# A state-space scan on one core: replication layout, a ring of two blocks, and a re-timed side schedule

## The reference, cut to what matters

```
x, z   = split(hidden @ in_proj.T)            # 512 channels each
u      = silu(conv4(x) + conv_b)              # causal, 4 taps
dt,B,C = split(u @ x_proj.T)                  # 16, 16, 16
delta  = softplus(dt @ dt_proj.T + dt_b)
dA     = exp(delta[..., None] * A)            # 512 channels x 16 states
dBu    = delta[..., None] * B[:, :, None, :] * u[..., None]
h      = dA * h + dBu                         # along 512 tokens
y      = sum_n(h * C)                         # over the 16 states
out    = ((y + u * D) * silu(z)) @ out_proj.T
```

## Time and profile before

| | us |
|---|---|
| median of 3 runs | 2438.59 |
| the profiled execution | 2434.86, with a span of 2433.1 |
| VectorE busy in the span | 1505.5 (62%) |
| TensorE (matmul) | 1817.2 (75%) |
| ScalarE, GpSimd | 1001.6 (41%), 941.8 (39%) |
| granted TensorE clock, mean | 0.838 |

### The profile page before, as it was taken

One profiled execution on the slowest core, in us unless ns is written; L12 is line 12 of the kernel. 1 busy time (PEld: TensorE's weight loads), 2 busy tenths in 40 slices (PEclk: granted clock), 3 DMA queues, 4 the chain that ended last, 5 costly groups with the idle time before them and its releaser, 6 DMA issues.

```text
span 2433.1 us, 21744 instructions
## 1 busy us (share of the span) xinstructions
PE 1817.2 (75%) x6696; PEld 770.0 (32%) x6696; DVE 1505.5 (62%) x1744; ACT 1001.6 (41%) x1542; POOL 941.8 (39%) x676
## 2 busy tenths in 40 slices
PE   6588989899999898761775766848758658478566
PEld 6344444435353535130212213213122122132212
DVE  6364646464656464411875876858768767587596
ACT  3134344343435252523453462543534534536332
POOL 2500000000000000104675675755756756556563
PEclk9899999999999999975777967869779668688666
DMA  4663544535252535116309036063090270540800
GB/s 173 201 134 59 130 67 120 78 109 90 97 99 88 99 100 90 57 42 146 71 18 206 12 80 153 10 142 83 10 207 18 61 174 10 125 91 1 202 14 9
DMA packets 104592, 223.80 MB, mean 92 GB/s; under 512 B 14177, under 2 KB 66530, under 8 KB 100818
## 3 DMA queue, kind: packets, MB, share of 16 engines
q1 hardware_dynamic: 101458, 214.69, 38.0%
q0 software_dynamic: 3072, 8.37, 1.0%
HBM read 169.56 MB, written 53.48 MB: 92 GB/s over the span
## 4 chain that ended last, share of the span: by engine, by line
PE 14%; issue 11%; DVE 10%; POOL 7%; POOLq 7%; DMA 5%; ACT 1%; DVEq 1%; SPq 1%; ACTq 0%
DVE ps L1440 6%; PE ps L1532 4%; POOL work L1181 4%; DMA rep<-rep_rows 3%; PE ps L1563 3%; DVE work L1446 3%; PE ps L1555 2%; POOLq L1152 2%; POOLq L1221 1%; POOL xn L1156 1%; PE ps L1565 1%; PE ps L1525 1%; DMA bc<-bc_rows 1%; POOLq L1168 1%; POOLq L1170 1%
## 5 line engine op out<-in xcount | busy, mean ns | idle before, releaser
L1440 DVE TENSOR_TENSOR_SCAN ps<-ps,work 128x1024 f32<-128x1024 f32 x256 | 586.3, 2290 | 318.7 <-POOL work L1181 282.4
L1181 POOL TENSOR_TENSOR work<-rep,bc 128x1024 f32<-128x1024 f32 x256 | 599.3, 2353 | 441.4 <-PE ps L1555 314.2
L1555 PE MATMUL ps<-work,pick 128*32 128x512 f32 x1024 | 325.9, 792 | 362.1 <-DVE work L1446 362.0
L1316 ACT ACTIVATE ps<-rep,a_neg 128x512 f32<-128x512 f32 x512 | 332.4, 681 | 640.2 <-DVE work L1446 599.0
L702 DVE TENSOR_REDUCE m<-ps 128x1 f32<-128x512 f32 x512 | 327.6, 686 | 163.6 <-PE ps L808 161.9
L625 ACT ACTIVATE prob<-ps 128x1024 f32<-128x1024 f32 x256 | 256.7, 1021 | 236.1 <-PE ps L832 234.0
L1446 DVE TENSOR_TENSOR work<-ps,bc 128x1024 f32<-128x1024 f32 x256 | 308.6, 1206 | 0.0
L1532 PE MATMUL ps<-xn_t,in_taps 128*128 128x510 f32 (+3 forms) x512 | 235.1, 615 | 13.4 <-ACT u L1254 12.4
L566 POOL TENSOR_TENSOR m_parts<-m,nil 128x16 bf16<-128x16 f32 x32 | 7.1, 222 | 604.0 <-DVE m L702 604.0
L808 PE MATMUL ps<-k_st,q_st 96*128 96x512 bf16 x512 | 184.6, 407 | 57.0 <-DMA k_st<-qk_parts 34.8
L1555 PEld LDWEIGHTS ps<-work,pick 128*32 128x32 f32 x1024 | 37.9, 121 | 590.9 <-DVE work L1446 526.9
(11 more groups left out here) (176 smaller groups left out, 1990.7 us busy)
## 6 DMA issues: line engine op xcount, KB each, us to landing
rep<-rep_rows SPq DMA_DIRECT2D x128, 512.0 KB, 16.0
w<-in_w SPq DMA_DIRECT2D x32, 1024.0 KB
rep_rows<-inputs SPq DMA_DIRECT2D x32, 512.0 KB, 6.3
bc<-bc_rows SPq DMA_DIRECT2D x128, 128.0 KB, 17.8
qk_parts<-parts SPq DMA_DIRECT2D x96, 128.0 KB
q_st<-qk_parts SPq DMA_DIRECT2D x96, 128.0 KB, 10.3
k_st<-qk_parts SPq DMA_DIRECT2D x96, 128.0 KB, 11.1
dispatch<-zeros SPq DMA_DIRECT2D x4, 1280.0 KB, 10.6
```

Source lines behind the costliest of these rows:

```text
L1181: nc.gpsimd.tensor_tensor(work[:, n % WS, :, :], rep[:, c, 2 * h:2 * h + 2, 1, :], bc[:, k, 0, :].unsqueeze(1).broadcast_to([P, 2, SEQ]), ...
L1316: e = nc.scalar.activation(state(n)[:, i, :], rep[:, c, 2 * h + i, 0, :], ACT.Exp, scale=a_neg[:, c, 2 * h + i, k:k + 1])
L1440: nc.vector.tensor_tensor_scan(s, s, work[:, n % WS, :, :].rearrange("p i t -> p (i t)"), 0.0, ALU.mult, ALU.add).then_inc(state_ready, 1)
L1555: x = nc.tensor.matmul(ps[j * CH:(j + 1) * CH, YB, :], pick[:, :], work[:, n % WS, i, :], start=False, stop=(n % PER_CHUNK >= PER_CHUNK - 2))
```

## The change

The tables get new positions and the kernel changes in these ways:
- **Layout.** Partition p now holds channel p // 4 and state group p % 4, so `pick` is `repeat` instead of `tile`, and each DMA of a load writes all 128 partitions. A load of `bc` is one DMA instead of four.
- **Ring.** `rep` has 2 blocks (`RS`) instead of 4. The load of chunk g waits until chunk g-2 has been used, and the loads stand in SP's queue at other places.
- **Drive places.** `WS` is 8 instead of 4.
- **Sums.** `sum_states(k)` takes pieces 2k and 2k+1 together, with one wait and one signal.
- **Halves.** The 8 matmuls of a chunk of `x` stand as 4 at q and 4 at q+1; the output projection goes by 4 tiles instead of 2 pairs.
- **Side chain.** Gather, weighing, adding, statistics and root of a batch are done one batch earlier (for b+2), so that the normalisation stands at q = 0. During batch 0, which has no such lead, all the positions are moved on by `LATE` = 5.
- **Attention.** `turn_rows(1)` and four of the second expert's eight `hide` stand ahead of the wait for `stacked`.

```
-WS = 4
+WS = 8
+RS = 2
+LATE = 5
+AHEAD = 4
...
-PE_AT = {"out": (1, 3), ... "turn_x": (6, 7), "x": (8, 10, 12, 14), "bc": 17, "dt": (19, 20, 21, 22), "z": (23, 24, 25, 26), ...
+PE_AT = {"turn_x": (0, 1), "out": (2, 3, 5, 6), ... "x": (7, 9, 11, 13), "bc": 16, "dt": (18, 19, 20, 21), "z": (22, 23, 24, 25), ...
-ACT_AT = {... "x": (11, 13, 15, 17), "silu_u": 17, ... "softplus": 24, ... "silu_z": 30}
+ACT_AT = {"normalise": 0, ... "x": (10, 12, 14, 16), "silu_u": 16, ... "softplus": 22, ... "silu_z": 29, "weigh": 24}
+DVE_AT = {"max": 2, "binade": 6, "statistics": 26}
+POOL_AT = {"down": 9, "grid": 14, "up": 17, "gather": 23, "add": 27, "input": 28, "root": 31}
...
                 def load_quad(f, k):
-                    for i in range(QUADS):
-                        n = QUADS * k + i
-                        sp.dma_start(bc[i * CH:(i + 1) * CH, k, :, :].rearrange("p r t -> p (r t)"),
-                                     rows[n:n + 1, :].broadcast_to([CH, 2 * SEQ])).then_inc(bc_loaded[k], 16)
+                    sp.dma_start(bc[:, k, :, :].rearrange("p r t -> p (r t)"),
+                                 rows.unsqueeze(0).broadcast_to([CH, QUADS, 2 * SEQ])).then_inc(bc_loaded[k], 16)
...
                 def load_inputs(f, c):
+                    g = f * DC + c
                     sp.wait_ge(rep_stored[c], f * 16 + 16)
-                    for i in range(QUADS):
-                        sp.dma_start(rep[i * CH:(i + 1) * CH, c, :, :, :].rearrange("p j r t -> p j (r t)"),
-                                     io["rep"][f % 2, c].rearrange("(j p) x -> p j x", p=CH)).then_inc(rep_loaded[c], 16)
+                    if g >= RS:
+                        sp.wait_ge(decay_ready, (g - RS + 1) * PER_CHUNK)
+                        sp.wait_ge(drive_ready, (g - RS + 1) * PER_CHUNK)
+                    for j in range(BLOCKS):
+                        rows = io["rep"][f % 2, c, j * CH:(j + 1) * CH, :]
+                        sp.dma_start(rep[:, g % RS, j, :, :].rearrange("p r t -> p (r t)"),
+                                     rows.unsqueeze(1).broadcast_to([CH, QUADS, 2 * SEQ])).then_inc(rep_loaded[g % RS], 16)
...
-                        pool.wait_ge(summed, n - WS + 1)
+                        pool.wait_ge(summed, (n - WS) // 2 + 1)
...
-                def sum_states(n):
-                    pe.wait_ge(read_ready, n + 1)
-                    for i in range(2):
-                        j = 2 * (n % 2) + i
-                        x = nc.tensor.matmul(ps[j * CH:(j + 1) * CH, YB, :], pick[:, :], work[:, n % WS, i, :], ...
+                def sum_states(k):
+                    pe.wait_ge(read_ready, 2 * k + 2)
+                    for n in (2 * k, 2 * k + 1):
+                        for i in range(2):
+                            j = 2 * (n % 2) + i
+                            x = nc.tensor.matmul(ps[j * CH:(j + 1) * CH, YB, :], pick[:, :], work[:, n % WS, i, :], ...
...
-"pick": np.tile(np.eye(CH, dtype=np.float32), (BLOCKS, 1))
+"pick": np.repeat(np.eye(CH, dtype=np.float32), QUADS, axis=0)
```

More of the change, by code:

```diff
@@ L866, in sequence @@
                         expert_out(0, j, range(HC))
+                        if j == 0:
+                            turn_rows(1)
+                    for h in range(AHEAD):
+                        hide(1, h)
                     pe.wait_ge(set_up, 1)
@@ L1007, in mix_block @@
         rep_stored = [sem(f"rep_stored_{c}") for c in range(DC)]
-        rep_loaded = [sem(f"rep_loaded_{c}") for c in range(DC)]
+        rep_loaded = [sem(f"rep_loaded_{c}") for c in range(RS)]
         dt_done = sem("dt_done")
@@ L1098, in _ @@
                 load(2)
-                spread(0)
+                store_rows(0)
+                for k in range(QUADS):
+                    load_quad(0, k)
+                for c in range(DC):
+                    store_inputs(0, c)
+                    if c == 0:
+                        load_inputs(0, 0)
                 for b in range(BATCH + 1):
+                    if b < BATCH:
+                        load_inputs(b, 1)
                     if b:
@@ L1385, in _ @@
                                 copy_quant(f, k)
-                        if q == ACT_AT["silu_z"]:
+                        if q == min(ACT_AT["silu_z"] + late, PIECES - 1):
                             silu_z(f)
@@ L1526, in in_proj, with in_proj_taps @@
                     x.then_inc(done, 1)
-                def in_proj_taps(bank, c, done):
-                    for s in range(TAPS):
+                def in_proj_taps(bank, c, taps, done):
+                    for s in taps:
                         for k in range(KD):
@@ new lines, in out_proj @@
+                def out_proj(b, t):
+                    o = ps[:, TB, (t % 2) * DM:(t % 2) * DM + DM]
+                    for c in range(DC):
+                        nc.tensor.matmul(o, sz[:, b % 2, c, t * P:(t + 1) * P], out_w[:, c, :], start=(c == 0), stop=False)
+                    for k in range(KD):
+                        nc.tensor.matmul(o, quant_t[:, b % 2, k, t * P:(t + 1) * P], fw_t[:, k, :], start=False, stop=False)
+                    nc.tensor.matmul(o, one_row, bias, start=False, stop=False)
+                    x = nc.tensor.matmul(o, sb["ident"][:, :], x2[:, b % XS, t, :], start=False, stop=True)
+                    if t % 2:
+                        x.then_inc(out_done, 1)
```

248 lines of the change are left out of this document (126 added, 122 removed).

## The result

The changed kernel takes 2224.4 us (median of 4 runs, 2220.3 to 2227.2) against 2438.1 us for the kernel before on the same chip: a ratio of 0.912, 95% interval 0.910 to 0.914. It is 214 us faster; 234 were forecast. The profiled execution took 2220.3 us with a span of 2218.5, which answers to the 2433.1 of the earlier trace rows.

The account below looks back on a forecast made before the run. VectorE was taken as the floor, busy 118.1 of 163.3 us a middle batch. Savings of 163 + 23 + 8 + 18 + 22 = 234 from 2434.9 gave 2201, 2205 with the median's 3.7; range 2152 to 2285.

Parts of the forecast that it names:

- attention: First part of the kernel: side work fills the wait for `stacked`, 2.8 us less a batch, 22 in 8 batches.
- the start: Second layer's first scan: `bc` loaded before the inputs are ready, first scan at 1134 instead of 1152, 18 us less.
- batch 0: Second layer's first batch: 17 us of late decays, gates and its end, so 135 us for 157.9, 23 less.
- six middle batches: Second layer: VectorE's 118.1 us plus 18 of stalls, 136 us a batch instead of 163.3, 163 less in six.
- head start: Attention, from the end of `expert_out` to the first probability matmul: 33.0 us instead of 35.8.
- at VectorE's pace: Attention's five steps without side work: set by two maxima of 0.69 us each, 7.0 us in all.
- attention gives nothing back: Rival: VectorE or the maxima's way through memory sets the end of the attention steps; 2227 us, chance 0.08.
- The walk: Piece-by-piece count of VectorE's stalls along a middle batch at 3.32 us a piece: late decays and gates, 18 us together.
- The drive waits: VectorE ahead of scans: 34.6 us a batch, 21 mid-batch and 13.6 at its end, go with 8 places and earlier loads.
- The seam: Batch end: first scan 15 us after the first store instead of 35, VectorE having 25 us of pieces; the stall goes.
- the ring: Rival: loads wait for a free block and each of 31 comes 9 us late; 2484 us, slower, chance 0.02.
- Halves: Chunks of `x` on TensorE: from batch 1 on no sum stands between the halves, so they cost and bring nothing.

Follow-up runs that it names:

- experiment 1: The changed kernel with the attention's second-expert output spread thinner, a quarter tile a step instead of a half: 2184.3 us, ratio 0.896.
- Experiment 2: The changed kernel with the attention's TensorE order of before, transposes and all `hide` behind the wait for `stacked`: 2223.9 us, ratio 0.913.
- experiment 4: The changed kernel with six drive places instead of eight, sums still in pairs: 2255.2 us, ratio 0.925.
- experiment 5: The changed kernel with the sums of one piece at a time instead of pairs, still eight drive places: 2257.8 us, ratio 0.927.
- experiment 3: The changed kernel with the old layout, each load of `rep` and `bc` writing 32 partitions, four loads a chunk: 2248.6 us, ratio 0.923.
- experiment 6: The kernel before with only the new layout, each load of `rep` and `bc` writing 128 partitions: 2368.2 us, ratio 0.973.
- experiment 7: The changed kernel with every chunk of `x` in one TensorE task instead of halves at q and q+1: 2227.1 us, ratio 0.914.

## Why the prediction was right, and where it was not

The parts of the sum, predicted and read from the two traces (spans 2433.1 and 2218.5):

| | predicted | measured |
|---|---|---|
| attention | -22 | -0.9 |
| the start | -18 | -20.4 |
| batch 0 | -23 | -18.9 |
| six middle batches | -163 | -166.4 |
| last batch | -8 | -8.9 |
| the tail | 0 | +0.8 |

- **Attention: the step that failed.** The prediction had the wait for `stacked` go, and the head start 2.8 us shorter; both came true (it was 4.65 us at the first probability matmul, in part since the five steps without side work took 6.0 us and not 7.0). What failed is the step from there to the sum, "22 in 8 batches", which lets the lead of the head start last to the end of the batch. The steps "at VectorE's pace" are steps in which TensorE idles, and after them its rows are those of the half clock for some 13 us (384.06 to 397.4), which gives the lead back: 0.9 us measured for the 22, which alone is as much as the 20 us by which the forecast is off. My bounds for this part went from nothing to 40 us "if the clock gains"; that it could lose did not come into the sum. The rival "attention gives nothing back" (2227 us) named the outcome and nearly the time, but by luck: it put it down to VectorE or the way through memory, and experiment 1 shows that neither held the batch. Experiment 2 confirms the size: nothing.
- **Middle batches: right in kind, and in size partly by luck.** Six at 135.6 us, 136 predicted. The walk had 1.9, 6.1, 7.2, 1.7 and 1.1 us; measured are 1.36, 5.61, 7.12, 3.98 and 1.13, with a gate at q = 17 of 1.17 that it lacked. The gate at q = 25 was mis-sized: TensorE waits at `z` for ScalarE, and I had counted only the projection. ScalarE and TensorE in this stretch:
```profile
1500.70 1.91 ACT L1306 ACTIVATE inputs<-inputs 128x2048 f32<-128x2048 f32 x1
1502.63 1.28 ACT L1333 ACT_TABLE_LOAD   x1
1503.92 2.52 ACT L1333 ACTIVATE ps<-rep,a_neg 128x512 f32<-128x512 f32 x4
1506.38 1.69 ACT L1252 ACTIVATE e_rows<-e_rows,gate_cur 128x256 f32<-128x256 f32 x4
1507.98 0.57 ACT L1310 ACTIVATE sz<-ps 128x512 f32<-128x512 f32 x1
...
1508.60 3.78 PE L1552 MATMUL ps<-xn_t,in_z 128*128 128x512 f32 x4 [6.82 <-ACT sz L1310]
```
Between the logarithm (L1306) and the copy of `z` (L1310) stand a table load, two decays and `weigh` (L1252, at q = 24), which is 1.7 us of the 6.8; no run moves `weigh`. That makes 20.4 us of stalls for 18.0, and VectorE's busy time is 2.3 us lower than I took it, 1.3 of them in the TENSOR_SCALAR. The errors cancel, and that the six batches come out within half a us of the forecast each owes something to it.
- **The drive waits went with the places**, as argued: none at 8, 19.0 us for `drive` and 20.8 for GpSimd's `to_grid` over the layer at 6 (experiment 4), 282.4 for `drive` at the 4 of the kernel before, where the order of the side work differs too. Of the pairs I had said that they save about half of the sums' TensorE time; experiment 5 finds the 16 us a batch, and that they act by `decay` and the gates.
- **The seam: right, and covered twice.** With the layout of before in the changed kernel (experiment 3) VectorE waits for `drive` at one seam of the seven, 8.7 us behind batch 0, where the changed kernel waits 7.1 for `decay`; so the new order of the loads and GpSimd's lead cover the seam without the layout; the new layout alone in the kernel before (experiment 6) takes 73 us off the waits for `drive`. The new order of the loads was not run without the lead. Loads in the new layout run at about 341 GB/s by experiment 3 and 366 by experiment 6, under the 389 that I took and well over 204. The Trainium skill, page "SBUF — State Buffer", section "Door 1: The DMA port swizzle", has 32 partitions reach half of the ports; 341 to 204 is a factor of 1.7, somewhat under its two. With a landing of 6.1 us the ring did not decide: in the changed kernel GpSimd waits for a `rep` load once, 2.5 us ahead of the first drive, and 19.8 us in nine times for `bc`, which its lead covers.
- **Halves: right**, nothing (experiment 7).
- **Batch 0: mis-sized.** 22.7 us of stalls for 17: 0.5 at scan 1, 5.6 in the gate at q = 17, 5.1 and 4.3 at scans 22 and 28, 7.1 at its end. The walk had the same two scans and the end, and one gate more.
- **Not shown: how the 214 us split.** Undone one by one, the layout is worth 24 us, two of the four new places 31 and the pairs 33, the attention and the halves nothing. The ring of two blocks, the side chain one batch earlier, and the new positions were never undone alone, so what they and the other two places brought is open.

## What to carry to other kernels

A wait that is taken away from TensorE is worth what the rows behind it show, not its length: look whether the freed time leaves it with steps that idle briefly, and at the rows behind them, where the same work cost 1.06 for 0.60 us here; spreading the same side work over nearly all steps turned 0 into 40 us, though two batches of eight still fell to the lower clock. Where several engines hand a side chain around under one bound engine, put a long ScalarE task and its neighbours at different places, and put TensorE tasks that wait for ScalarE behind the sums that the bound engine needs next. A change that brings nothing alone (the logarithm apart) may be worth 16 us once the wait that takes it back is gone, so try it again after each step.

## What the runs showed of the hardware

**TENSOR_SCALAR of VectorE waits inside itself for GpSimd.** No list of waits shows it; only the duration and the moment of the end do. In the changed kernel, VectorE and GpSimd on the timeline:
```profile
1428.48 5.15 POOL L1192 TENSOR_TENSOR work<-rep,bc 128x1024 f32<-128x1024 f32 x2
1428.55 2.29 DVE L1460 TENSOR_TENSOR_SCAN ps<-ps,work 128x1024 f32<-128x1024 f32 x1
1430.75 0.68 DVE L1440 TENSOR_SCALAR e_rows<-xn 128x1024 int32<-128x1024 int32 x1
1431.51 2.68 DVE L1443 TENSOR_SCALAR e_rows<-e_rows 128x1024 f32<-128x1024 f32 x1
```
The first goes through between two GpSimd operations, which take 5.15 us together where two usually take 4.65. The second ends at 1434.19, 0.56 us after GpSimd's second, although its own work is 0.70 us where nothing stands beside it. In six of the seven batches of the changed kernel it takes 2.67 or 2.68 us, and in the seventh, where GpSimd has finished when it starts, 0.70; in the kernel before L1420 takes 1.98 us each time and ends 0.54 to 0.56 us after a GpSimd operation. Scans and VectorE's products with `bc`, which have one operand in PSUM, take 2.29 and 1.21 us beside GpSimd as well. By the Trainium skill, page "SBUF — State Buffer", section "SBUF: two separate sides", VectorE and GpSimd share a port pair as an exclusive lock, held for a whole instruction, which VectorE needs for an operation in a two-port mode or with two inputs in SBUF. These rows agree with a lock; in which mode the TENSOR_SCALAR ran, no row shows. Over the second layer the three TENSOR_SCALAR of a batch (21 in all) took 33.5 us in the kernel before, 25.0 in the changed kernel and 38.1 in experiment 3, and which of them is long changes from kernel to kernel, so a few us of each difference above are a matter of how they happen to meet.
